# A 32-sequence language-model tower on one core: the first stage re-sorted, and the split of w1 moved into the fill of the second

## What is computed

```
cont  = window3_mean(pca_lookup[x]) @ proj_w + proj_b
fused = concat(emb[x], cont) @ fus_w + fus_b
h     = layernorm(fused) * ln_g + ln_b                      # B=32, S=128, D=256
h    += attention(layernorm(h))       # 16 heads of 64, inner residual and layernorm
h    += routed_ffn(layernorm(h))      # 16 experts of 64, top 2, half of each sequence per expert
```

## Time and profile before

| what | value |
|---|---|
| median of 3 runs | 556.43 us (555.6 to 559.4) |
| the profiled execution | 557.69 us |
| its span, first to last instruction | 555.7 us |
| TensorE, VectorE, ScalarE, GpSimd busy | 93%, 81%, 66%, 69% of the span |
| TensorE's mean granted clock | 0.992 of full speed |

### The profile page before, as it was taken

The page is one execution under the profiler, slowest core; times in us unless marked ns, Lnnn a source line. Parts: engine busy times, 40 slices in busy tenths (PEclk is TensorE's granted clock), DMA queues, the critical chain, the costliest instruction groups (busy, mean ns, idle before and its releaser), DMA issues. The chain is left out here.

```text
span 555.7 us, 16203 instructions
## 1 busy us (share of the span) xinstructions
PE 516.9 (93%) x6063; PEld 385.9 (69%) x6063; DVE 448.6 (81%) x1013; ACT 367.2 (66%) x776; POOL 382.2 (69%) x508
## 2 busy tenths in 40 slices
PE   4996879999999999999999999878999999999874
PEld 2894757777777777777777777643457676676664
DVE  5676668888888988888888888977976988887775
ACT  1588668787877878787778778616675555555440
POOL 4000876787878878787878788942177887898783
PEclk9997999999999999999999999999999999999999
DMA  6900000000000000000000000000733044172011
GB/s 195 351 4 0 2 2 3 4 3 1 4 3 2 4 3 2 4 4 2 4 3 4 2 3 2 3 0 2 156 87 86 21 122 104 23 170 54 28 40 58
DMA packets 11905, 21.74 MB, mean 39 GB/s; under 512 B 4668, under 2 KB 9780, under 8 KB 10164
## 3 DMA queue, kind: packets, MB, share of 16 engines
q1 hardware_dynamic: 11828, 20.71, 13.6%
HBM read 16.24 MB, written 4.33 MB: 37 GB/s over the span
## 5 line engine op out<-in xcount | busy, mean ns | idle before, releaser
L792 POOL TENSOR_TENSOR s_pl<-s_pf,s_ph 128x512 f16<-128x512 f32 x128 | 147.0, 1159 | 6.9 <-ACT s_ph L890 6.7
L979 DVE TENSOR_REDUCE s_mx<-ps 128x4 f32<-128x512 f32 x128 | 83.7, 676 | 29.0 <-PE ps L1120 28.9
L770 PE MATMUL ps<-s_xt_all,s_w1s 128*128 128x512 f16 x384 | 87.8, 379 | 2.2 <-ACT s_ub L1432 1.6
L1587 PE MATMUL ps<-s_w2s,s_hid 128*128 128x256 f16 x768 | 88.9, 273 | 0.0
L884 ACT ACTIVATE s_pf<-ps 128x512 f32<-128x512 f32 x128 | 76.6, 601 | 17.3 <-PE ps L1133 17.2
L1587 PEld LDWEIGHTS ps<-s_w2s,s_hid 128*128 128x128 f16 x768 | 75.1, 98 | 10.9
L890 ACT ACTIVATE s_ph<-s_pf 128x512 f16<-128x512 f32 x128 | 77.2, 637 | 0.0
L1166 PE MATMUL ps<-s_zh,s_cth 128*128 128x256 f16 x256 | 69.8, 273 | 0.0
L1166 PE MATMUL ps<-s_zh,s_ctl 128*128 128x256 f16 x256 | 69.8, 273 | 0.0
L1166 PE MATMUL ps<-s_zl,s_cth 128*128 128x256 f16 x256 | 69.8, 273 | 0.0
L770 PEld LDWEIGHTS ps<-s_xt_all,s_w1s 128*128 128x128 f16 x384 | 37.4, 98 | 41.5 <-ACT s_ub L1432 2.1
(11 more groups left out here) (231 smaller groups left out, 1241.3 us busy)
## 6 DMA issues: line engine op xcount, KB each, us to landing
s_rep<-picks SPq DMA_DIRECT2D x14, 512.0 KB, 6.1
s_stage<-in_w SPq DMA_DIRECT2D x2, 1024.0 KB, 13.8
out<-s_ot_a SPq DMA_DIRECT2D x16, 128.0 KB, 1.7
out<-s_lg SPq DMA_DIRECT2D x16, 128.0 KB, 1.7
s_stage<-in_wq SPq DMA_DIRECT2D x1, 1024.0 KB, 5.0
s_stage<-in_wk SPq DMA_DIRECT2D x1, 1024.0 KB, 6.6
s_stage<-in_wv SPq DMA_DIRECT2D x1, 1024.0 KB, 8.3
s_stage<-in_wo SPq DMA_DIRECT2D x1, 1024.0 KB, 10.0
```

Of the source, the lines that this page charges most:

```text
L770: mm = nc.tensor.matmul(hidden_bank(n)[:], w1s[:, wp, c, j * P:(j + 1) * P], xt_all[:, GB * g:GB * (g + 1), xp, c, :], start=(k == 0), sto ...
L792: nc.gpsimd.tensor_tensor(flat(pl[:, b % 2, 4 * j:4 * j + 4, :]), pf[:, j, :], flat(ph[:, b % 2, 4 * j:4 * j + 4, :]), ALU.subtract).then_ ...
L979: nc.vector.tensor_reduce(mx[:, b % 2, c:c + 4], A[ab][:].rearrange("p (h k) -> p h k", h=4), AX.X, ALU.max).then_inc(max_done[hf][ab], 1)
L1587: mm = nc.tensor.matmul(zb[b % 4], hid[:, g % 2, hp, j, t * P:(t + 1) * P], w2s[:, wp, j, :], start=False, stop=(j == NJ - 1 and hp == 1))
```

## The change

In the first stage:

- GpSimd clears 256 columns each of `nb` and `uf` in place of 2048.
- The three loads that the table needs (`fus_w`, `embT`, `fus_b`) are issued on ScalarE's queue, ahead of its Sqrt table load; SP no longer issues them.
- The roots: ScalarE takes the Sqrt straight from `red` and from `t3` with scale and bias in the activation; the Newton step has four operations in place of five; `sig` is worked out later (`scales`).
- The split token factors are kept once (512 columns for eight sequences). TensorE writes both halves of a transposed bank, with two matmuls of 64 weight columns each in place of one of 128.
- VectorE evicts the fourth bank of every eight sequences (`ut_last`), ScalarE the other three. The lists of ScalarE, VectorE and TensorE behind that are put in another order.
- The first three of `table(0)`'s eight chunks take the place of twelve fillers; other fillers go from 19 to 7, 6 to 4 and 36 to 16.

In the fill of the second block: ScalarE's Exp table load and the upper part of w1 are moved there, the table load ahead of `token_rows` 9 and 10 of the step -3, w1's upper part behind them. GpSimd splits w1 last and waits for ScalarE's part (`w1_top`).

```
 # sync                                     # gpsimd
-sp.wait_ge(cleared, CLEARED["lhs"])        -memset(nb[:], 0.0)
-sp.dma_start(lhs_t[...], d["embT"])        +memset(nb[:, :, 2 * V:UD], 0.0)
-sp.dma_start(fus_w[:], d["fus_w"])         -memset(uf[:], 0.0)
-sp.dma_start(fus_b[:], d["fus_b"])         +memset(uf[:, :, R2:UD], 0.0)
 # scalar
+act.dma_start(fus_w[:], d["fus_w"]).then_inc(in_fus, 16)
+act.wait_ge(cleared, CLEARED["lhs"])
+act.dma_start(lhs_t[:, 0:KC, 0:V], d["embT"]).then_inc(in_fus, 16)
+act.dma_start(fus_b[:], d["fus_b"]).then_inc(in_fus, 16)
 nc.scalar.preload_act_table(ACT.Sqrt)
...
-act.wait_ge(in_w12, 48)
-nc.scalar.activation(both(w1s[:, 0]), stage2[:, 0, :], ACT.Copy, scale=W_SCALE)
-root(0, v1, q1)
+root_1()     # waits for red_ok; Sqrt(red / D + eps)
 table(1)
-root(1, v2, q2)
+root_2()     # waits for t3; Sqrt(t3 / D + s_eps)
 table(2)
...
 g_hi()
-nc.scalar.preload_act_table(ACT.Exp)
 u_hi(0); u_hi(1)
-u_hi(2); z_hi(0); u_cols(0, 0..3); u_hi(3); z_hi(1); u_cols(1..3, 0..3); z_hi(2); z_hi(3)
+z_hi(0); u_cols(0, 0..2); u_hi(2); z_hi(1); u_cols(1, 0..2); u_hi(3); z_hi(2)
+u_cols(2, 0..2); z_hi(3); u_cols(3, 0..2)
 # vector, behind roots()
 u_rows(0); u_rows(1); u_lo(0); u_rows(2); u_lo(1)
-z_lo(0); u_rows(3); u_lo(2); g_lo(); u_lo(3); z_lo(1); z_lo(2); z_lo(3)
+u_rows(3); u_cols(0); g_lo(); u_lo(2); z_lo(0); u_cols(1); u_lo(3); z_lo(1)
+u_cols(2); scales(); z_lo(2); z_lo(3); u_cols(3)
 # tensor
-keep_going(19) ... keep_going(6) ... keep_going(12)
-quads(0); quads(1); table(0); quads(2); quads(3)
+keep_going(7) ... keep_going(4) ... table(0, range(3))
+quads(0); quads(1); table(0, range(3, HD)); quads(2); quads(3)
 table(1); table(2); gram(); z_part(0); z_part(1)
-keep_going(36); u_cols(0..3); z_part(2); z_part(3)
+keep_going(16); u_cols(0); u_cols(1); z_part(2); z_part(3); u_cols(2); u_cols(3)
...
-matmul(UT_BANKS[n][:, x:x + P], both(src[...]), identh[:], start=True, stop=True)
+for ab in range(2):
+    matmul(UT_BANKS[n][ab * UD:(ab + 1) * UD, x:x + P], src[:, b, :], identh[:], start=True, stop=True)
 # gpsimd, second block
-scale_and_lo(w1 ...)       # between wg and w2
+pool.wait_ge(w1_top, 1)
+scale_and_lo(w1 ...)       # behind wg, w2 and b2
 # scalar, second block, step -3
 q_hi(i + 4, 1)
+nc.scalar.preload_act_table(ACT.Exp)
 token_rows(9); token_rows(10)
+act.wait_ge(in_w12, 48)
+nc.scalar.activation(both(w1s[:, 0]), stage2[:, 0, :], ACT.Copy, scale=W_SCALE).then_inc(w1_top, 1)
```

More of the change, by code:

```diff
@@ L284, in _, with root_1, root_2 @@
                 nc.scalar.activation(mr[0:UD, :], mbo[:], ACT.Copy, scale=Y_SCALE).then_inc(mr_ok, 1)
-                def root(n, v, r):
-                    act.wait_ge(v_ok, n + 1)
-                    nc.scalar.activation(r[:], v[:], ACT.Sqrt).then_inc(sqrt_ok, 1)
+                def root_1():
+                    act.wait_ge(red_ok, NQ)
+                    nc.scalar.activation(q1[:], both(red[:, :, 0:1]), ACT.Sqrt, bias=eps_x[:], scale=1.0 / D).then_inc(sqrt_ok, 1)
+                def root_2():
+                    act.wait_ge(seps_ok, 1)
+                    act.wait_ge(root_step, T3_STEP)
+                    nc.scalar.activation(q2[:], t3[:], ACT.Sqrt, bias=s_eps[:], scale=1.0 / D).then_inc(sqrt_ok, 1)
                 def table(n):
@@ L334, in _ @@
                 g_hi()
-                nc.scalar.preload_act_table(ACT.Exp)
                 u_hi(0)
                 u_hi(1)
+                z_hi(0)
+                for n in range(3):
+                    u_cols(0, n)
                 u_hi(2)
-                z_hi(0)
-                for n in range(4):
-                    u_cols(0, n)
+                z_hi(1)
+                for n in range(3):
+                    u_cols(1, n)
                 u_hi(3)
[L343 to L346, removed]
                 z_hi(2)
+                for n in range(3):
+                    u_cols(2, n)
                 z_hi(3)
+                for n in range(3):
+                    u_cols(3, n)
             @block.vector
@@ L493, in _ @@
                 u_lo(1)
+                u_rows(3)
+                u_cols(0)
+                g_lo()
+                u_lo(2)
                 z_lo(0)
-                u_rows(3)
-                u_lo(2)
-                g_lo()
+                u_cols(1)
                 u_lo(3)
-                for n in range(1, 4):
-                    z_lo(n)
+                z_lo(1)
+                u_cols(2)
+                scales()
+                z_lo(2)
+                z_lo(3)
+                u_cols(3)
             @block.tensor
@@ L556, in _, with table @@
                 mm.then_inc(cs_ready, 1)
-                def table(n):
+                def table(n, chunks=range(HD)):
                     pe.wait_ge(in_w[n], 32)
@@ L563, in table @@
                         pe.wait_ge(qkv_ok, 2)
-                    for c in range(HD):
+                    for c in chunks:
                         for kc in range(KC):
@@ L636, in _ @@
                 pe.wait_ge(prod_ok, 2 * NQ)
-                keep_going(36, psum[2][:, 0:FREE])
-                for g in range(NQ):
-                    u_cols(g)
+                keep_going(16, psum[2][:, 0:FREE])
+                u_cols(0)
+                u_cols(1)
                 z_part(2)
                 z_part(3)
+                u_cols(2)
+                u_cols(3)
         one.close()
```

83 lines of the change are left out of this document (44 added, 39 removed).

## The result

| what | forecast | measured |
|---|---|---|
| time, median (18 executions of each kernel) | 549.0 us, range 545.5 to 554.0 | 553.95 us, against 557.52 before |
| ratio to before | 0.987 | 0.9934 [0.9919, 0.995] |
| gain | 7.4 us | 3.6 us |

The kernel before came out at 557.52 in its 18 executions, 1.1 above the median of three that the forecast started from.

A forecast was written before the change was run, and what follows sets the result against it. The first stage was taken as a chain changing engine, with TensorE full from about 83 us. First-stage gains of 10.6 us less 3.2 in the fill gave -7.4, so 556.4 became 549.0 us, range 545.5 to 554.0.

The forecast's parts named there:

- The start (-1.9): First stage's start: shorter GpSimd clears free VectorE's first cast, gain 2.4 us, less 0.5 for loads on ScalarE's queue.
- Rival E: At the start: cast not freed, or loads take the gain; +1.9 us, 551; chance 0.08 together with small additions.
- Fillers (-1.6) and quadratic forms (-0.4): First stage, TensorE: 7 fillers end before VectorE's table work, 1.6 us; `quads(2)` comes sooner, 0.4 us of VectorE idle saved.
- rival D: First stage: with fewer fillers TensorE's clock doesn't rise, tables run at 1.2 GHz; slower, about 562 us; chance 0.05.
- Roots (-1.3): First stage, from `red` to `u_rows`: three VectorE operations go and both roots come one hop earlier, 1.3 us sooner.
- To the split (-6.0): First stage up to `u_hi(0)`: earlier gains that reach it, plus the table load gone, start it at 34.8, not 40.83.
- to the end (-4.6): From the split to the first stage's end: ScalarE's list shrinks from 14.1 to 10.0 us; a further 4.6 us sooner.
- rival B: First stage's transposes: 64-column weight loads don't overlap, eight sequences take 3.2 us; +4.5 us, 553.5; chance 0.12.
- The fill (+3.2): Second block's fill: GpSimd waits for w1's late upper part, so `values(0, 0)` and everything behind it come 3.2 us later.
- Rival A: Fill: slack behind `values(0, 0)` hides the delay, only ScalarE's 1.1 us are lost; 547, or 546 with overlapping pairs; chance 0.13.
- Behind the fill (0): From `values(0, 0)` to the kernel's end: no change forecast, 477.5 us against 477.51 before.
- Rival C: Fill: TensorE's clock falls after the longer wait, costing up to 3.4 us; 551 to 552.5; chance 0.12.

The follow-up runs named there:

- loads_on_sp: Changed kernel with its three table loads back on SP's queue, behind the band's load: 553.69 us, ratio 0.9941.
- loads_behind_ids: Changed kernel with ScalarE's three loads issued behind its Sqrt table load and the landing of the ids: 554.31 us, ratio 0.9937.
- fillers_19_6: Changed kernel with 19 and 6 early fillers in place of 7 and 4: 551.37 us, ratio 0.991.
- fillers_20: Changed kernel with 20 fillers in place of 7 ahead of the table's transposes: 553.39 us, ratio 0.9938.
- old_fillers: Changed kernel with early fillers as before (19, 6 and 12) and table(0) whole behind the first quadratic forms: 553.31 us, ratio 0.9927.
- w1_in_stage1: Changed kernel with w1's upper part back in the first stage and GpSimd's old order, Exp table load still in the fill: 550.39 us, ratio 0.9892.

## Why the prediction was half right

**The start (-1.9): this step failed.** The cast was freed as forecast, 2.4 us were there; but I took 0.5 for the loads on the second queue and bounded them by 1.3, from 512 KB at 394 GB/s. `iota` landed 1.9 us late. The bound was wrong because it priced the bytes at the rate of a full stretch, which the start doesn't reach: from 1.0 to 5.4 us the changed kernel's mean is 172 GB/s. loads_on_sp and loads_behind_ids, with the cast at 3.35, show that these loads are the cause. And I asked only what delays the cast, not what would be last once it is gone: `fus_b` at 8.3. Measured: the table's matmuls 0.45 sooner (9.44 to 8.99), with 1.2 as the most that any order tried had. Rival E was this, and its 1.9 less gain came in nearly whole (1.45).

**Fillers (-1.6) and quadratic forms (-0.4): right in kind.** `quads(0)` moved by 1.73, of which 0.45 came in from the start: 1.28. That seven fillers "end first" is not what the profile has: at 1.2 GHz they end 0.1 us behind VectorE, and where they do end first, TensorE waits 1.5 us and the clock falls. The sum put the loss of the fillers at nothing and left it to rival D. From `quads(0)` to `red` are 10.23 us in place of 10.77, and no VectorE idle is left ahead of `quads(2)`.

**Roots (-1.3): right in kind.** From `red` to `u_rows(0)` 3.99 us, before 4.94: -0.95. The first reciprocal starts 0.46 behind `red`, where I had 0.3.

**To the split (-6.0) and to the end (-4.6).** The first is -4.4, short by 1.6, nearly all of it the start's 1.45. The second is -5.2: the narrow transposes overlap in pairs. In the changed kernel's timeline of TensorE, each row being one pair:

```profile
38.13 0.25 PE L618 MATMUL ps<-s_identh,s_uh 128*64 128x128 f16 x2 [0.23 <-DVE s_ul L477]
38.19 0.25 PE L618 MATMUL ps<-s_identh,s_ul 128*64 128x128 f16 x2
38.24 0.25 PE L618 MATMUL ps<-s_identh,s_uh 128*64 128x128 f16 x2
...
38.97 0.25 PE L618 MATMUL ps<-s_identh,s_ul 128*64 128x128 f16 x2
```

A pair every 0.056 us, eight sequences in 1.1: my lower bound (1.0), not the 2.1 that I took, and far from rival B's 3.2. The 128-column transposes of before came one every 0.055 us, so a pair costs what one matmul did. The Trainium skill ("TensorEngine Tiling (Array Packing)", Restrictions) says that column tiling disables the fast weight load. The trace doesn't speak against that (a weight load of 64 columns takes 0.110 us here, one of 128 columns took 0.098 before); what fails is the step from there to B, for the loads overlap and their length is not on the path.

**The fill (+3.2): right as a mechanism, and to 0.1 us where the clock stays up.** In fillers_19_6, fillers_20 and old_fillers it is 23.97 to 23.98, so +3.3; w1 is 2.5 of it (w1_in_stage1 has 23.14, against 25.63 with the same slow start), the table load the other 0.8. Rival A is out. In the profile of the changed kernel 1.7 more come from a spell at the fill's start. So it is with GpSimd's idle time ahead of w1's scaling: 4.41 us in fillers_19_6, where the forecast had 4.2, and 6.06 with the spell. The drain that the Trainium skill ("ScalarE: Activation LUTs", What ACT_TABLE_LOAD costs) adds to a table load is not there: ScalarE's next operation starts at the end of the load.

```profile
60.38 1.28 ACT L963 ACT_TABLE_LOAD   x1
61.67 1.57 ACT L938 ACTIVATE s_h<-ps,s_sig 128x256 f32<-128x256 f32 x4
```

**Behind the fill (0).** Rival C came on top of my sum instead of in its place: the rest is 1.1 us longer in the changed kernel, and in the pair of profiles above the wait with its spell costs 2.2. This step failed as well: the sum put the clock behind the wait at nothing. I had its mechanism and its size (up to 3.4) and gave it 0.12 as an alternative, though nothing in it excludes the forecast; with 2.2 us for it in the sum the forecast would have been 551, and with the start's 1.45 about 552.5. That it is in the median is not shown: four of nine profiles with the wait have no such spell, and filling the wait moved no median.

**Sum over the spans.** -9.6 + 5.0 + 1.1 = -3.5, against -10.6 + 3.2 = -7.4: 1.0 short in the first stage (1.6 up to the split, 0.6 given back by evictions and transposes), 1.8 in the fill, 1.1 behind it. In this one profile more of the missing gain is clock (some 2.8) than work.

## What to carry to other kernels

An idle engine isn't a free place for a producer: w1's split moved from a stage where it hid completely to one where GpSimd, and behind it TensorE's list, waited for it, and undoing that alone was worth 2.7 to 3.9 us. Where a change makes TensorE wait, put the work behind the wait at half the clock into the sum with its chance (here five profiles of nine), and not only among the rivals. Fillers that look too many in one profile may be what covers a wait in another execution, whose clock rose sooner. When a first wait of a start is removed, look for the second (here a load of one row) before counting the gain, and a large load on a second queue delays the small ones that everything waits for.

## What the runs showed of the hardware

- TensorE's clock stayed at 0.50 for 30.7 us in which it was busy without a pause (busy 10.00 of 10 in three stretches), with fp32 matmuls of 64 columns most of the time, and rose only while the bf16 fillers from 48.55 on ran. In all six profiles with seven fillers and an early rise the clock fell at 17.5 to 19.5 us, two to three microseconds behind a wait of 1.5 us; in two of them it came back after 6.7 us, in the middle of the same work.
- A wait of 3.5 us in thin work was followed by 6.8 us at 1.2 GHz in five of nine profiles, and in none of eight without it.
- The same first stage ended 2.6 us apart in two executions (block 2 at 46.44 and 49.03) by when the clock first rose, before 12.4 us or behind 15.
- `iota` landed before 3.4 us with the large loads behind it on either queue, and at 5.4 with `fus_w` (512 KB) on ScalarE's queue issued at 0.74; `fus_b`, 1 KB and the smallest of the three, landed last and held the table at 8.31 on SP's queue, with 1.34 us of waiting.
- Two fp16 matmuls with 64 weight columns each, on the two column halves, took the time of one with 128: a pair every 0.056 us.
